# Moving the mixing, the rounding of x and two rounds of weight sums to later places in a hand-made order of work (one core)

## The reference

```
x = x + attn(cond(x, mix_w, itok_B_0_15))      # cond: W = mix_w[condition of the batch]; einsum('bct,bcd->bdt', x, W)
x = x + ffn(cond2(x, ...))                     # low-rank adapted linear layer, then a linear layer
# attn: 32 query heads, 8 key/value heads of 128; q = rms(h Wq'), k = rms(h Wk'), v = h Wv';
#       softmax(q k' / sqrt(128) + causal slope * distance) v, then Wo
```

## Time and profile before

| | |
|---|---|
| median of 3 runs | 2375.29 us (2374.58 to 2379.8) |
| the profiled execution | 2375.95 us |
| its span, first to last instruction | 2374.0 us |
| TensorE busy in the span | 2344.8 us |
| VectorE busy | 1776.3 us |
| ScalarE busy | 1464.5 us |
| mean granted TensorE clock, as a share of full | 0.997 |

### The profile page before, as it was taken

The page is one execution under the profiler, slowest core; times in us unless marked ns, Lnnn a source line. Parts: engine busy times, 40 slices in busy tenths (PEclk is TensorE's granted clock), DMA queues, the critical chain, the costliest instruction groups (busy, mean ns, idle before and its releaser), DMA issues.

```text
span 2374.0 us, 33429 instructions
## 1 busy us (share of the span) xinstructions
PE 2344.8 (99%) x11706; PEld 1961.6 (83%) x11706; DVE 1776.3 (75%) x2930; ACT 1464.5 (62%) x3625; POOL 285.1 (12%) x336
## 2 busy tenths in 40 slices
PE   8999999999999999999999999999999999999998
PEld 6877888888888888888888888888888888888886
DVE  6777969696847878787846777777876696969691
ACT  4246767576625857576824857576844676767660
POOL 1222010101011001010021101010021101010111
PEclk9999999999999999999999999999999999999999
DMA  6774434442542242423443242423244242423250
GB/s 254 265 262 187 160 134 155 147 135 73 195 150 89 86 145 74 148 72 134 143 153 116 72 160 71 160 72 124 97 172 144 81 150 70 151 80 139 73 197 36
DMA packets 88440, 316.16 MB, mean 133 GB/s; under 512 B 12716, under 2 KB 13228, under 8 KB 87124
## 3 DMA queue, kind: packets, MB, share of 16 engines
q1 hardware_dynamic: 70292, 247.14, 30.1%
q0 software_dynamic: 16256, 62.92, 7.2%
q10 hardware_dynamic: 1728, 3.98, 0.5%
HBM read 282.54 MB, written 31.46 MB: 132 GB/s over the span
## 4 chain that ended last, share of the span: by engine, by line
PE 94%; DVE 3%; DMA 1%; issue 1%; ACT 0%; POOL 0%; ACTq 0%; POOLq 0%; DVEq 0%
PE main L1041 80%; PE qt_bank L1202 3%; PE s_bank L1218 3%; PE s_bank L1219 2%; PE pv_bank L1239 1%; PE pv_bank L1238 1%; PE pt_bank L1226 1%; PE pt_bank L1041 1%; DVE ring L1511 1%; DVE setup L1511 0%; PE qt_bank L1139 0%; PE s_bank L1139 0%; DMA acc<-in_x 0%; DMA t_scratch<-sums 0%; DMA mask<-in_masks 0%
## 5 line engine op out<-in xcount | busy, mean ns | idle before, releaser
L1041 PE MATMUL main<-ring,act_hi 128*128 128x512 f32 x3584 | 1148.4, 402 | 0.4 <-DVE ring L1511 0.3
L1041 PEld LDWEIGHTS main<-ring,act_hi 128*128 128x128 f32 x3584 | 641.5, 189 | 114.3 <-issue 3.1
L1041 PE MATMUL main<-ring,act_lo 128*128 128x512 f32 x1792 | 701.7, 392 | 0.0
L1041 PE MATMUL main<-ring,lefts 128*128 128x512 f32 x2688 | 625.9, 391 | 0.0
L1041 PEld LDWEIGHTS main<-ring,lefts 128*128 128x128 f32 x2688 | 499.9, 188 | 101.5
L1511 DVE TENSOR_TENSOR ring<-raw,ring 128x1024 fp32r<-128x1024 f32 x448 | 550.5, 1233 | 41.1 <-ACT ring L1249 38.9
L1249 ACT ACTIVATE ring<-raw 128x1024 fp32r<-128x1024 f32 x448 | 472.0, 1056 | 172.0 <-PE main L1041 149.6
L1041 PEld LDWEIGHTS main<-ring,act_lo 128*128 128x128 f32 x1792 | 336.9, 188 | 74.9
L1850 POOL TENSOR_TENSOR rstd<-mean,half 128x4 f32<-128x4 f32 (+1 forms) x192 | 174.0, 906 | 1535.1 <-DVE mean L1636 1535.0
L1382 ACT ACTIVATE sq<-main 128x128 f32<-128x128 f32 x640 | 169.3, 277 | 76.1 <-PE main L1041 72.2
L1410 ACT ACTIVATE prob<-score,peak 128x64 f32<-128x64 f32 x512 | 136.1, 336 | 98.1 <-DVE peak L1694 97.4
(11 more groups left out here) (168 smaller groups left out, 2554.3 us busy)
## 6 DMA issues: line engine op xcount, KB each, us to landing
raw<-in_wq SPq DMA_DIRECT2D x128, 512.0 KB, 4.3
raw<-t_scratch SPq DMA_DIRECT2D x128, 512.0 KB, 3.2
raw<-in_wo SPq DMA_DIRECT2D x96, 512.0 KB, 3.2
raw<-in_wkv SPq DMA_DIRECT2D x64, 512.0 KB, 3.9
sums<-in_wo POOLq DMA_DIRECT2D x32, 512.0 KB, 7.6
t_scratch<-sums POOLq DMA_DIRECT2D x32, 512.0 KB, 4.1
raw<-f_scratch SPq DMA_DIRECT2D x32, 512.0 KB, 4.9
acc<-in_x POOLq DMA_DIRECT2D x16, 512.0 KB, 4.1
```

What stands on the lines that cost most here:

```text
L1041: mm = eng.matmul(bank, a, b, start=start and n == 0 and m == 0, stop=stop and n == len(terms) - 1 and m == 2, skip_group_check=further)
```

## The change

Three lines of numbers change, and no instruction is added or removed.

```
-          mix_split=7.4, mix=9.8, reload=5.1,
+          mix_split=8.4, mix=10.5, reload=5.1,
...
-KEYS_AT = dict(mixing=(2.8, 3.4, 3.9), queries=(3.8, 4.4, 4.9), projection=(4.8, 5.4, 5.9))
+KEYS_AT = dict(mixing=(3.8, 4.35, 4.38), queries=(3.8, 4.4, 4.9), projection=(4.8, 5.4, 5.9))
...
-ROUND_AT = (0.5, 18.5, 35, 104, 180)
+ROUND_AT = (0.5, 20.5, 37, 104, 180)
```

## The result

The changed kernel takes 2391.39 us (median of 5 runs, 2389.59 to 2393.07), the kernel before beside it 2376.64 us (5 runs). The ratio is 1.0061, 95% interval 1.0047 to 1.0075: the change costs about 0.6%. The profiled execution is the shortest of the five, 2389.59 us with a span of 2387.4, which is 13.4 more than the 2374.0 of before.

What follows compares the result with a forecast made beforehand. TensorE, busy 2344.8 of 2374.0 us (99%), was taken to bound the kernel. The mixing's 9.65 plus the rounds' 2.3 made 11.95 us, added to the median of 2375.29 for 2387.2, range 2380 to 2394.

Steps and rivals of the forecast that it cites:

- Need of a mixing, 4.42: From a mixing's first matmul until the `kv` 0 step reading it may begin: 4.27 + 0.15 = 4.42 us.
- The waits, 3.45 a border: TensorE waits for four mixings at each border: 0.51 + 1.06 + 0.94 + 0.94 = 3.45 us, 10.35 for three.
- The key transpose still stands inside C's and D's rooms, only later in them.: Mixings C and D at each border keep a key transpose before their reader; rooms 3.48 us, a wait of 0.94 each.
- The `k_t` wait at the second border goes, -0.7.: At the second border, mixing D's 0.66 us wait for `k_t` goes, since keys now stand ahead of x; 0.7 off.
- The first moved round, 1.45: Block 0, first moved round of sums: the scaling starts 1.45 us later; the wait at 206.29 grows to about 1.9.
- the second, 0.85: Block 0, second moved round of sums: the scaling starts 0.85 us later, where TensorE already waited 0.79; net 0.85.
- The 4.11 wait and its half clock left as they are.: At 180.04 in block 0, `rstd` stands behind a load POOL holds 3.54 us; wait and half clock stay unchanged.
- Rival: the clock falls.: Waits at borders or in block 0 lower the clock: 2390.6 us if once, 2397.4 at every border; chance 0.08.
- Rival: a second hold on POOL.: After the first moved round, loads wait up to 3.5 us for stores to land; some 2394 us; chance 0.02.

Runs made afterwards that it cites:

- waits for single banks: Changed kernel, but each quarter of a `kv` or `q` step waits only for the mixing bank it reads: 2379.77 us, ratio 1.0017 to the kernel before.
- keys alone: Kernel before with only the key transposes moved, to 3.8, 4.35, 4.38 quarters from 2.8, 3.4, 3.9: 2381.11 us, ratio 1.0016.
- keys left early: Kernel before with the mixing and x's rounding moved as in the change, key transposes and rounds of sums left in place: 2385.93 us, ratio 1.0041.
- rounds alone: Kernel before with only the two rounds of sums moved, to 20.5 and 37 quarters from 18.5 and 35: 2379.50 us, ratio 1.0014.
- loads behind `rstd`: Kernel before with the two rounds of sums at 22.5 and 39 quarters, so that one `rstd` stands ahead of the loads: 2372.69 us, ratio 0.9987.
- rounds placed with x early: Kernel before with only two rounds moved: loads at 22.5 and 34 quarters, sums 2.4 and 1.7 sooner, x's rounding at 7.4: 2369.54 us, ratio 0.9972.
- mixing, x and keys alone: Changed kernel with the rounds of sums put back, so only the mixing, x's rounding and the key transposes are moved: 2388.88 us, ratio 1.0050.
- x late: Kernel before with x's rounding alone one quarter later, at 8.4; mixing, keys and rounds as before: 2382.41 us, ratio 1.0024.

## Why the prediction was right, and where it fell short

The forecast was slower, 2387.2 in a range of 2380 to 2394; the median is 2391.39. Of the 4.2 between them, 1.35 is the kernel before, whose median is 2376.64 over five runs in place of 2375.29 over three. The rest is the loss itself, 14.75 by the medians where 11.95 was forecast. The profiled pair differs by only 13.4, since the first wait and its half clock were 1.4 cheaper in that execution.

- **Need of a mixing, 4.42.** Right: 4.49, 4.42, 4.42, 4.42. The run with waits for single banks shows that the wait for the last bank is what turns the lost quarter into time.
- **The waits, 3.45 a border.** Nearly right. They show in the trace as 0.40, 1.02, 0.81 and 0.81, because the idle time is read from modelled ends; the start of the step tells the time lost. The first border is 4.73 longer, of which the gain's wait takes 1.0; the 3.7 that is left is 0.3 over the forecast. No wait won back another.
- **"The key transpose still stands inside C's and D's rooms, only later in them."** This step failed. It asked only what the transpose does on TensorE. The third one's lower part comes late on DVE, and the fourth step's mean, values and gain are queued behind it: 0.84 of idle time and 1.0 of time lost at each border, 3.0 us over three. It is most of what the borders cost beyond the forecast (12.9 against 9.65). The runs with keys alone and with keys left early show it from both sides.
- **The `k_t` wait at the second border goes, -0.7.** It is gone, and the second border got 1.2 back rather than 0.7. The cause that the forecast gives, keys behind x on DVE, isn't shown. In the three runs that leave the order at the borders as it was (rounds alone, loads behind `rstd`, rounds placed with x early) the second border has no such wait above 0.13, while the third has one of 0.46 to 0.57 for `act_lo`; their three borders together are as long as before (118.65 to 119.21 against 118.98). That the -0.7 stood for one small wait that all these executions have somewhere, and the change has nowhere, is luck as far as the place goes.
- **The first moved round, 1.45, and the second, 0.85.** Right in the net: -0.34 + 0.67 + 1.14 = 1.47 for the first, 1.16 - 0.38 = 0.78 for the second. That the waits of 1.93 and 1.95 met the forecast's "about 1.9" is luck. By its own numbers TensorE comes 0.34 earlier to the first, so that a net of 1.45 needs 0.79 + 1.45 + 0.34 = 2.6 of waiting; the 2.6 came, but 0.67 of it at a score ahead. For the second they give 0.79 + 0.85 = 1.6, and the trace has 1.95 with 0.38 less at a score.
- **The 4.11 wait and its half clock left as they are.** Right in kind: 3.60 in the profile, 3.67 with the rounds alone. The price of 3.4 for the half clock was too high: 1.5 of the 6.8 us lay inside the wait, and the clock cost 2.7. The hold on POOL stayed, and the run with the loads at 22.5 quarters shows that `rstd` behind the held load was its cause.
- **Rival: the clock falls.** Not at the borders: 1.00 over 60 us with four waits of 0.4 to 1.0 in it. In block 0 it can: with the rounds alone it fell behind both waits of 1.9, in the changed kernel's profile behind neither, and with the keys late behind one of 0.98. Whether that is part of the 1.8 us between the profiled execution and the median isn't shown, since only one execution of each is profiled. The Trainium skill, page "TensorE: Matmul & The Clock Gate", section "A second HAM failure mode: psum-queue depth-cycling", has the clock swing where short idles between groups of matmuls are frequent enough. The fifteen idles of 0.4 to 1.0 at the borders, each more than 7 us of matmuls behind the one before it, did not bring it down; how frequent is enough the page doesn't say, so the trace neither bears it out nor refutes it.
- **Rival: a second hold on POOL.** It came, but cost nothing. The loads of the second moved round were held 1.14, 0.65, 1.21 and 1.43 us; the last was issued at 209.96, and `rstd` behind it at 210.54 was in time.

## What to carry to other kernels

When work is moved by a quarter, work out the room between its first instruction and its reader against the time that its chain takes; where TensorE is 99% busy, what is lacking is lost one for one, and a wait for the last of several banks makes the chain longer than the reader needs. For each moved step follow the results through every engine's queue: the cost of the late keys was not where they are read, but in the next step's operations behind them. Before a sum or a load is placed, ask which steps leave its engine free, and which small operation that somebody waits for stands behind a DMA that may be held.

## What the runs showed of the hardware that was not expected

The clock's answer to one and the same wait is not the same in each execution. Behind the wait near 180 it was at half for 6.8 us in the profile of before (4.11), of mixing, x and keys alone (4.09) and of the waits for single banks (3.94), and for 3.4 in those of the change (3.60), the rounds alone (3.67) and keys late (3.45), but also in those of mixing late (4.09) and x late (4.06). So a wait of 4.1 had both lengths behind it. After waits of 1.9 it fell in two of two places with the rounds alone, in one of two with the loads behind `rstd`, and in none of two in the changed kernel and with waits for single banks: three of eight. One profile doesn't give the price of such a wait: it is the wait alone, or the wait and 1.7 us more. Nor is a short wait safe: one of 0.98, in block 0 with the keys late, had 3.4 us of half clock behind it.

A held load isn't a wait of the kernel: in the run with the loads at 22.5 quarters POOL was held up to 1.95 us for a load, in the second moved round of the changed kernel four times in a row, and TensorE waited for none of them. It counts only where an `rstd` that is needed soon stands behind it.
